# Mamba scan over its own decays in PSUM, with some multiplications by C moved to GpSimd

## Chip, cores and metric

The kernel runs on one core of a Trainium2 chip. The metric is the device time of one execution in microseconds. A core has five engines that run their own instruction queues in order and meet through semaphores: TensorE (PE), VectorE (DVE), ScalarE (ACT), GpSimd (POOL) and SyncE (SP, which issues DMAs here). Data lie in SBUF or in PSUM, the matmul output buffer.

## The reference, cut to what matters

The model is a tower of four blocks. The first is a three-layer Mamba beside a bidirectional LSTM, on 64 sequences of S = 33 tokens with D = 128 features. The inner width is 256 channels, so two halves of 128 partitions, and each channel has 16 states. For every layer:

```python
def step(h, inp):
    dt_t, B_t, C_t, u_t = inp
    dA = jnp.exp(dt_t[..., None] * A)
    h = dA * h + (dt_t * u_t)[..., None] * B_t[:, None, :]
    y = jnp.einsum('bcn,bn->bc', h, C_t)
    return (h, y)
```

Then `y + u * Dp`, times `silu(z)`, through `out_proj` and a layer norm. The other blocks (expert feed-forward layers, attention, a state space layer, an LSTM mixture of experts) are not touched by the change.

## The kernel before

All of this is in `mamba_lstm` (L389). The 64 sequences of a layer are cut into five items of 13, 13, 13, 13 and 12 sequences (858 or 792 columns for both channel halves together), so three layers make 15 items, j = 0 to 14. Each item goes through its 16 states, k = 0 to 15, and g = 16 j + k counts states over the whole loop, 240 of them. For one state:

- ScalarE computes the decays dA = exp(dt * A) into one of two PSUM buffers, `dA[:, g % 2]`, in two activations, one for each half (`decay`, L1036). It writes columns 1 to 32 of each sequence; column 0 holds a zero from one memset at the start (L1280), which restarts the recurrence at each sequence. Decay g waits for scan g - 2 (`h_ready`), which frees the buffer.
- GpSimd computes dBu = du * B into one of two SBUF buffers (L1346), also after scan g - 2.
- VectorE runs the recurrence over all columns in one `tensor_tensor_scan` from dA and dBu into `hst`, a ring of HR = 5 SBUF buffers (`scan`, L1251), and multiplies that buffer in place with C (`weigh`, L1261). Both operands of the multiplication lie in SBUF. The order on VectorE is scan(g), weigh(g - 1), scan(g + 1), weigh(g) and so on.
- TensorE adds the product into `py` in PSUM with two identity matmuls (`add`, through the helper line L573). A scan that reuses a ring buffer waits for the addition five states earlier.

B and C rows, replicated over the partitions, come by DMA from SP's queue, two states at a time, in rings of NBS = 4 buffers. A buffer of C is loaded again when `weighed` shows that its states are done.

Other work is written out by hand between the states, by the value of k. On VectorE: `soften` (L1193, L1196, L1201: e, dt, du of item j + 1) and `back` (L1215) at k = 8, `gate` (L1209, yz) at k = 1, the LSTM's `lstm_c` (L1223, L1225, L1228: ig, act3, cz) at k = 1, 5, 9 and `lstm_h` (L1235) at k = 2, 6, 10. On ScalarE, in this order within a state: decay(g), then `lstm_cell` (tc = tanh(c), L1018, at k = 3, 7, 11, which waits for VectorE's cz), `lstm_gates` (k = 2, 6, 10), `lstm_keep` (k = 4, 8, 12), the softplus steps of item j + 1, the layer norm, and `project`, which at k = 11 loads the SiLU tables (L876), runs three SiLUs (L878, L880, L882) for item j + 2 and loads the exponential's tables again (L883). The LSTM runs three time steps in each of the items 1 to 11 (`LSTM_ITEMS` = 11), so items 12 to 14 have no LSTM work, and items 13 and 14 no `project`. The GpSimd loop has dBu alone, beside eight small weight products (L1320); at k = 10 it waits for `soften` and `back`.

The order of VectorE's and ScalarE's loops around the change:

```python
for g in range(NI * DST):
    j, k = g // DST, g % DST
    scan(g)
    if g >= 1:
        weigh(g - 1)
```

Of the kernel before, what the change touches and what calls it, by code (L numbers as in the profile page):

```python
# [10 lines left out]
ALU = mybir.AluOpType  # L11
ACT = mybir.ActivationFunctionType
# [3 lines left out]
S = 33  # L16
# [356 lines left out]
LOG_KAPPA = -26 * 0.6931471805599453  # L373
PER_ITEM = 3
LSTM_ITEMS = S // PER_ITEM


def item(j):
# [5 lines left out]
def by_seq(ap):  # L384

    return ap.rearrange("p (b s) -> p b s", s=S)


def mamba_lstm(nc, cst, consts, mdct_dram, frames_dram, w_dram, cw_dram, lstm_dram, xn, m, hT):  # L389

    with ExitStack() as ctx:
        def sb(name, shape, dt=F32):
            return sbuf(nc, ctx, name, shape, dt)
# [5 lines left out]
        wop = sb("wop", [128, NL, 2, 128])  # L399
        negA = sb("negA", [128, NL, 2 * DST])  # L400
        edge = sb("edge", [128, 6])
        u = sb("u", [128, 2, 2, SCW])
        sz = sb("sz", [128, 3, 2, SCW])
        dt = sb("dt", [128, 2, 2, SCW])
# [39 lines left out]
                      "z_gated xd_ready xd_done rows_stored"))  # L444
        (d_ready, mag_ready, d_read, e_ready, capped, w_ready, sq_w_ready, ln_ready, low_logged, low_ready, high_ready, dt_done, du_done) = ctx.enter_context(
            stage(nc, "d_ready mag_ready d_read e_ready capped w_ready sq_w_ready ln_ready low_logged low_ready high_ready dt_done du_done"))
        (dA_zeroed, dBu_ready, dA_ready, h_ready, weighed, y_added, y_gated) = ctx.enter_context(
            stage(nc, "dA_zeroed dBu_ready dA_ready h_ready weighed y_added y_gated"))
        (wop_ready, wop_kept, cent_ready, cent_kept, sq_ready, var_ready, var_read, rstd_ready, m_scaled, m_done) = ctx.enter_context(
            stage(nc, "wop_ready wop_kept cent_ready cent_kept sq_ready var_ready var_read rstd_ready m_scaled m_done"))  # L450
        (diag_ready, bias_set, lw_ready, gates_ready, gated, prods_ready, c_ready, tc_ready, r_ready, hs_kept, fused, fused_added) = ctx.enter_context(
# [60 lines left out]
        @block.sync  # L512
        def _(sp):
            wih_d, whh_d, b_d, fw_d, fb_d = lstm_dram

            def load_cw(l):
                if l == 1:
                    sp.wait_ge(built_first, DCV)
                else:
                    sp.wait_ge(built, DCV * (l - 1))  # L520
                sp.dma_start(cw[:, :, :], cw_dram[l].unsqueeze(0).broadcast_to([128, DCV, DIN])).then_inc(cw_loaded, 16)

            def store(j):
                l, at, n = item(j)
                sp.wait_ge(xd_done, j + 1)
                sp.dma_start(bc_rows[j % 3, :, 0:n], xd[DTR:DTR + 2 * DST, j % 2, 0:n]).then_inc(rows_stored, 16)

            def rows(j, first, k):
                l, at, n = item(j)
                return bc_rows[j % 3, first + BG * k:first + BG * k + BG, 0:n].unsqueeze(0).broadcast_to([128, BG, n])  # L530

            def load_frames(c):
                per = NB // NCH
                sp.dma_start(blocks[:, c * per:(c + 1) * per, :],
                             frames_dram.rearrange("p (b s) -> p b s", b=NB)[:, c * per:(c + 1) * per, :]).then_inc(f_loaded[c], 16)

            sp.dma_start(mdct, mdct_dram.rearrange("p (k n) -> p k n", k=2)).then_inc(mdct_loaded, 16)
            load_frames(0)
            load_frames(1)
            sp.dma_start(w[:, 0, :], w_dram[0]).then_inc(w0_loaded, 16)  # L540
            sp.dma_start(cw[:, :, :], cw_dram[0].unsqueeze(0).broadcast_to([128, DCV, DIN])).then_inc(cw0_loaded, 16)
            load_frames(2)
            load_frames(3)
            for l in range(1, NL):
                sp.dma_start(w[:, l, :], w_dram[l]).then_inc(w_loaded, 16)
            for dst, src in ((wih[:, :, :, :].rearrange("p g d h -> p (g d h)"), wih_d), (lb[:, 0, :], b_d[0]), (lb[:, 1, :], b_d[1]),
                             (fw[:, :, :], fw_d), (fb[:, :], fb_d)):
                sp.dma_start(dst, src).then_inc(l_loaded, 16)
            sp.wait_ge(l_zeroed, 1)
            for d in range(2):  # L550
                sp.dma_start(whh[d * H2:(d + 1) * H2, :, d, :], whh_d[d]).then_inc(l_loaded, 16)
            store(0)
            for j in range(NI):
                l, at, n = item(j)
                for k in range(NGR):
                    if k == 0:
                        sp.wait_ge(rows_stored, 16 * (j + 1))
                    q = NGR * j + k
                    if q >= NBS:
                        sp.wait_ge(dBu_ready, BG * (q - NBS + 1))  # L560
                    sp.dma_start(Bs[:, q % NBS, :, 0:n], rows(j, 0, k)).then_inc(b_loaded[q % NBS], 16)
                    if q >= NBS:
                        sp.wait_ge(weighed, BG * (q - NBS + 1))
                    sp.dma_start(Cs[:, q % NBS, :, 0:n], rows(j, DST, k)).then_inc(c_loaded[q % NBS], 16)
                    if k == (1 if j else 2) and j + 1 < NI:
                        store(j + 1)
                    if k == 2 and j in (0, NSC):
                        load_cw(l + 1)

        @block.tensor  # L570
        def _(pe):
# [137 lines left out]
            def add(g):  # L709
                j, k = g // DST, g % DST  # L710
                l, at, n = item(j)
                if k == 0:
                    if j >= 1:
                        pe.wait_ge(y_gated, j)
                    else:
                        pe.wait_ge(z_gated, 1)
                    pe.wait_ge(u_gated, j + 1)
                    pe.wait_ge(diag_ready, 2 * (l + 1))
                    for h in range(2):
                        mm(py[:, h, 0:n], diag[:, l, h, :], u[:, j % 2, h, 0:n], start=True, stop=False)  # L720
                pe.wait_ge(weighed, g + 1)
                for h in range(2):
                    last = mm(py[:, h, 0:n], cst["ident"], hst[:, g % HR, h * n:h * n + n], start=False, stop=(k == DST - 1))
                last.then_inc(y_added, 1)
# [90 lines left out]
        def _(act):  # L815
# [211 lines left out]
            def decay(g):  # L1027
                j, k = g // DST, g % DST
                l, at, n = item(j)
                if k == 0:  # L1030
                    act.wait_ge(dt_done, j + 1)
                if g >= 2:
                    act.wait_ge(h_ready, g - 1)
                for h in range(2):
                    o = by_seq(dA[:, g % 2, h * n:h * n + n])[:, :, 1:S]
                    last = a(o, by_seq(dt[:, j % 2, h, 0:n])[:, :, 1:S], ACT.Exp,  # L1036
                             scale=negA[:, l, h * DST + k:h * DST + k + 1])
                last.then_inc(dA_ready, 1)
# [102 lines left out]
        def _(dve):  # L1141
# [102 lines left out]
            def scan(g):  # L1244
                j = g // DST
                l, at, n = item(j)
                if g >= HR:
                    dve.wait_ge(y_added, g - HR + 1)
                dve.wait_ge(dBu_ready, g + 1)
                dve.wait_ge(dA_ready, g + 1)  # L1250
                v.tensor_tensor_scan(hst[:, g % HR, 0:2 * n], dA[:, g % 2, 0:2 * n], dBu[:, g % 2, 0:2 * n], 0.0, ALU.mult,  # L1251
                                     ALU.add).then_inc(h_ready, 1)

            def weigh(g):
                j, k = g // DST, g % DST
                l, at, n = item(j)
                q = g // BG
                dve.wait_ge(h_ready, g + 1)
                dve.wait_ge(c_loaded[q % NBS], 16 * (q // NBS + 1))
                h = hst[:, g % HR, 0:2 * n].rearrange("p (a n) -> p a n", a=2)  # L1260
                v.tensor_tensor(h, h, Cs[:, q % NBS, k % BG, 0:n].unsqueeze(1).broadcast_to([128, 2, n]),  # L1261
                                ALU.mult).then_inc(weighed, 1)

            keep_tokens(0)
# [17 lines left out]
            for g in range(NI * DST):  # L1282
                j, k = g // DST, g % DST
                scan(g)
                if g >= 1:
                    weigh(g - 1)
                if j == 0 and k in (3, 7, 11):
                    scale_unit(2 + k // 4)
                if 1 <= j <= LSTM_ITEMS:
# [21 lines left out]
        def _(pool):  # L1311
            g_ = nc.gpsimd

            def build(l, r):
# [4 lines left out]
                    pool.wait_ge(x_ready, 2 * NSC * (l - 1))  # L1319
                g_.tensor_tensor(wt[:, l % 2, r, :], W(l, "wi", 0, DIN), cw[:, r, :], ALU.mult).then_inc(built, 1)  # L1320

            for at, value in enumerate((BELOW_ONE, KAPPA / 2, -KAPPA * KAPPA / 6, LOG_KAPPA, CAP, KAPPA * KAPPA / 12)):
                g_.memset(edge[:, at:at + 1], value).then_inc(edge_set, 1)
            g_.memset(whh[:, :, :, :], 0.0).then_inc(l_zeroed, 1)
            pool.wait_ge(w0_loaded, 16)
            pool.wait_ge(cw0_loaded, 16)
            for r in reversed(range(DCV)):
# [3 lines left out]
            for g in range(NI * DST):  # L1331
# [12 lines left out]
                if g >= 2:  # L1344
                    pool.wait_ge(h_ready, g - 1)
                g_.tensor_tensor(dBu[:, g % 2, 0:2 * n].rearrange("p (a n) -> p a n", a=2), du[:, j % 2, :, 0:n],  # L1346
                                 Bs[:, q % NBS, k % BG, 0:n].unsqueeze(1).broadcast_to([128, 2, n]), ALU.mult).then_inc(dBu_ready, 1)
                if j in (1, NSC + 1) and k in (2, 4, 6, 8):
                    build(l + 1, k // 2 - 1)

# [2762 lines left out]
```

## Time and profile before

| what | value |
|---|---|
| median of 3 runs | 2124.9 us (2123.95 to 2128.16) |
| the profiled execution's own time | 2123.37 us |
| its span, first to last instruction | 2121.5 us |
| granted TensorE clock, mean share | 0.943 |
| PE busy | 1841.3 us (87%) |
| DVE busy | 1634.3 us (77%) |
| ACT busy | 1323.1 us (62%) |
| POOL busy | 1015.5 us (48%) |
| scans (L1251), 240 | 458.3 us |
| multiplications with C (L1261), 240 | 247.3 us |
| dBu on GpSimd (L1346), 240 | 589.2 us |
| decays (L1036), 480 activations | 269.9 us |

The loop over the 240 states takes the span from about 35 us to 803 us. A timeline row gives the start in us, the duration in us, engine, line, operation, the tile written and the tiles read, the shape (partitions x elements), how many instructions were merged, and in brackets the idle time of the engine before it and what ended it. Consecutive instructions of one engine overlap a little at their ends, so the distance from start to start is shorter than the duration. A row of grouped instructions ends with busy us, mean ns of one, and the idle time ahead of the group.

### The profile page before, as it was taken

How to read it: one execution, taken by the hardware profiler on the slowest of the kernel's cores; microseconds unless marked ns; L12 is line 12 of the kernel's file. 1: busy time of each engine (PE TensorE's matmuls, PEld its weight loads, DVE VectorE, ACT ScalarE, POOL GpSimd, SP SyncE). 2: the span in 40 equal slices, each digit the busy share in tenths (PEclk: the TensorE clock that was granted, in tenths of full speed). 3: DMA queues.
4: the chain of work that ended last, by engine and by line, in shares of the span. 5: the costliest groups of instructions: out<-in, count | busy, mean ns of one | idle time of the engine just before them, and what ended most of it. 6: DMA issues, size and time to landing. Idle time of an engine off the chain costs nothing. (4 is left out here: it accounts for less than half of the span.)

```text
span 2121.5 us, 49383 instructions
## 1 busy us (share of the span) xinstructions
PE 1841.3 (87%) x19527; PEld 1346.4 (63%) x19527; DVE 1634.3 (77%) x2595; ACT 1323.1 (62%) x2681; POOL 1015.5 (48%) x782
## 2 busy tenths in 40 slices
PE   8899889898888778987878787897798799999999
PEld 4444444444443335445567787676776599999999
DVE  5999999999999994768475442546544689998996
ACT  6988887778876643123544444342646488888886
POOL 3787777777777881100037777200630133333333
PEclk9999999999999998997879999898988799999999
DMA  5444444444445441600148889303720411112000
GB/s 191 128 137 140 132 145 134 136 140 133 136 140 144 133 115 41 155 9 1 28 127 270 253 264 249 86 0 116 245 65 12 191 66 66 66 66 77 7 7 7
DMA packets 98037, 241.63 MB, mean 114 GB/s; under 512 B 15024, under 2 KB 48320, under 8 KB 95504
## 3 DMA queue, kind: packets, MB, share of 16 engines
q1 hardware_dynamic: 89120, 218.12, 33.4%
q0 software_dynamic: 7680, 15.74, 3.2%
q10 hardware_dynamic: 1008, 4.62, 0.6%
q8 instruction: 155, 2.54, 0.5%
q14 instruction: 74, 0.61, 0.1%
HBM read 226.25 MB, written 12.19 MB: 112 GB/s over the span
## 5 line engine op out<-in xcount | busy, mean ns | idle before, releaser
L1346 POOL TENSOR_TENSOR dBu<-du,Bs 128x858 f32<-128x858 f32 (+1 forms) x240 | 589.2, 2457 | 184.4 <-DVE hst L1251 95.0
L573 PE MATMUL py<-hst,ident 128*128 128x429 f32 (+1 forms) x960 | 405.9, 551 | 78.6 <-DVE hst L1261 78.3
L1251 DVE TENSOR_TENSOR_SCAN hst<-dA,dBu 128x858 f32<-128x858 f32 (+1 forms) x240 | 458.3, 1910 | 6.6 <-ACT dA L1036 4.0
L573 PEld LDWEIGHTS py<-hst,ident 128*128 128x128 f32 x960 | 178.1, 197 | 269.3 <-DVE hst L1261 150.4
L1036 ACT ACTIVATE dA<-dt,negA 128x416 f32<-128x416 f32 (+1 forms) x480 | 269.9, 596 | 115.2 <-DVE hst L1251 113.5
L3671 POOL TENSOR_TENSOR hm<-h,mw 128x264 f32<-128x264 f32 x128 | 89.8, 701 | 390.7 <-DVE h L3651 390.7
L1261 DVE TENSOR_TENSOR hst<-hst,Cs 128x858 f32<-128x858 f32 (+1 forms) x240 | 247.3, 1030 | 0.0
L3542 PE MATMUL pg<-xm,wi 128*128 128x66 f16 x6144 | 214.3, 195 | 8.2 <-issue 6.8
L3542 PE MATMUL pg<-hs,wh 128*128 128x66 f16 x6144 | 217.5, 194 | 2.9 <-issue 2.9
L3542 PEld LDWEIGHTS pg<-xm,wi 128*128 128x128 f16 x6144 | 201.6, 98 | 12.8 <-issue 7.5
L3542 PEld LDWEIGHTS pg<-hs,wh 128*128 128x128 f16 x6144 | 203.8, 98 | 6.5 <-issue 3.1
L3068 ACT ACTIVATE eh<-ph,wb 128x128 f32<-128x128 f32 x384 | 109.4, 368 | 133.5 <-PE ph L2941 133.5
L3592 ACT ACTIVATE pg<-bz 128x1188 f32<-128x1188 f32 x128 | 149.1, 1166 | 6.2 <-PE pg L3537 2.2
L3641 DVE TENSOR_TENSOR prod<-z 128x528 f32<-128x528 f32 x128 | 111.7, 873 | 16.7 <-ACT z L3602 16.3
L2910 POOL DMA_INDIRECT xi<-token_rows,take x96 | 93.5, 974 | 44.9 <-issue 40.3
L3006 DVE COPY yo<-po 128x128 f32<-128x128 f32 x96 | 28.0, 291 | 106.3 <-PE po L2951 106.3
L2915 POOL DMA_INDIRECT expert_rows<-yo,give x96 | 94.9, 988 | 30.7 <-issue 25.9
L2941 PE MATMUL ph<-xT,wb 128*128 128x128 f32 x768 | 104.5, 280 | 1.8 <-DVE xT L3000 1.8
L3601 ACT ACTIVATE z<-pg,scale 128x528 f32<-128x528 f32 x128 | 88.1, 688 | 24.1 <-PE pg L3542 23.1
L2951 PE MATMUL po<-wb,eh 128*128 128x128 f32 x768 | 102.0, 277 | 0.0
L2349 POOL DMA_INDIRECT xi<-token_rows,take x24 | 25.4, 1057 | 157.5 <-issue 156.2
L2941 PEld LDWEIGHTS ph<-xT,wb 128*128 128x128 f32 x768 | 95.3, 195 | 2.8 <-DVE xT L3000 2.8
(600 smaller groups left out, 3471.5 us busy)
## 6 DMA issues: line engine op xcount, KB each, us to landing
wb<-sf_w SPq DMA_DIRECT2D x96, 514.0 KB, 5.3
Bs<-bc_rows SPq DMA_DIRECT2D x96, 429.0 KB, 4.6
Cs<-bc_rows SPq DMA_DIRECT2D x96, 429.0 KB, 3.5
mw<-route_weights SPq DMA_DIRECT2D x8, 2112.0 KB, 10.0
wb<-gf_w SPq DMA_DIRECT2D x24, 514.0 KB, 4.9
Bs<-bc_rows SPq DMA_DIRECT2D x24, 396.0 KB, 5.2
Cs<-bc_rows SPq DMA_DIRECT2D x24, 396.0 KB, 4.3
mb<-route_masks SPq DMA_DIRECT2D x8, 1088.0 KB, 12.7
```

What stands on the lines that cost most here:

```text
L573: return nc.tensor.matmul(out, weight, moving, **kw)
L1036: last = a(o, by_seq(dt[:, j % 2, h, 0:n])[:, :, 1:S], ACT.Exp, scale=negA[:, l, h * DST + k:h * DST + k + 1])
L1251: v.tensor_tensor_scan(hst[:, g % HR, 0:2 * n], dA[:, g % 2, 0:2 * n], dBu[:, g % 2, 0:2 * n], 0.0, ALU.mult, ALU.add).then_inc(h_ready, 1)
L1261: v.tensor_tensor(h, h, Cs[:, q % NBS, k % BG, 0:n].unsqueeze(1).broadcast_to([128, 2, n]), ALU.mult).then_inc(weighed, 1)
L1346: g_.tensor_tensor(dBu[:, g % 2, 0:2 * n].rearrange("p (a n) -> p a n", a=2), du[:, j % 2, :, 0:n], Bs[:, q % NBS, k % BG, 0:n].unsqueeze( ...
L2915: pool.indirect_dma_start(ys, bass.IndirectOffsetOnAxis(ap=give[:, d:d + 1], axis=0), yo[:, d % UN, :], None).then_inc(given[d % UN][0], 16)
L2941: last = nc.tensor.matmul(ph[:, j % 2, f * ST:(f + 1) * ST], wb[:, j % UN, f * 128:(f + 1) * 128], xT[:, j % UN, :], start=True, stop=True)
L2951: last = nc.tensor.matmul(po[:, j % 2, 0:D], eh[:, j % 3, f, :], wb[:, j % UN, F + f * D:F + (f + 1) * D], start=(f == 0), stop=(f == FC - 1))
L3068: last = nc.scalar.activation(eh[:, j % 3, f, :], ph[:, j % 2, f * ST:(f + 1) * ST], act_fn, bias=wb[:, j % UN, W1 + W2 + f:W1 + W2 + f + 1])
L3542: return nc.tensor.matmul(pg[q][:, bank, c:c + CB], (wh if u else wi)[:, wp, q * HE + e, GO[z_] * D:(GO[z_] + 1) * D], rhs, start=False, s ...
L3592: a(pg[q][:, :, 0:PERB * CB], bz[:, q, :, :], ACT.Copy).then_inc(seeded[q], 1)
L3641: link(v.tensor_tensor(prod[:, q, :, :], z[:, q, 0:2, :], z[:, q, 3:5, :], ALU.mult))
```

## The change

Each state gets a kind. "S" stays as it was. In "D" the scan writes over its decays in PSUM, VectorE multiplies from there into the `hst` buffer directly after the scan, and ScalarE, before it writes the next decays into that buffer, waits for the multiplication and puts the zeros back with a copy of 26 elements for each partition. In "P" the scan writes `hst` as before and GpSimd multiplies it in place, after the dBu of two states later. Items 1 to 11 have D at k = 8, 9, 12, 13 and P at k = 10, 14. Items 12 to 14 repeat D, D, P over k = 2 to 13. All else is S, so there are 68 D, 34 P and 138 S. `weighed` now counts VectorE's multiplications and `weighed_pool` GpSimd's. TensorE's addition waits for the one that applies, SP's load of C for both.

```diff
+IN_LSTM = {8: "D", 9: "D", 10: "P", 12: "D", 13: "D", 14: "P"}
+
+def kind(g):
+    j, k = g // DST, g % DST
+    if j <= LSTM_ITEMS:
+        return IN_LSTM.get(k, "S") if j >= 1 else "S"
+    return "DPD"[k % 3] if 2 <= k < DST - 2 else "S"
...
@@ SP
-                        sp.wait_ge(weighed, BG * (q - NBS + 1))
+                        sp.wait_ge(weighed, by_vector(BG * (q - NBS + 1) - 1))
+                        if by_gpsimd(BG * (q - NBS + 1) - 1):
+                            sp.wait_ge(weighed_pool, by_gpsimd(BG * (q - NBS + 1) - 1))
...
@@ TensorE, add(g)
-                pe.wait_ge(weighed, g + 1)
+                if kind(g) == "P":
+                    pe.wait_ge(weighed_pool, by_gpsimd(g))
+                else:
+                    pe.wait_ge(weighed, by_vector(g))
...
@@ ScalarE, decay(g)
-                if g >= 2:
+                if g >= 2 and kind(g - 2) == "D":
+                    act.wait_ge(zero_set, 1)
+                    act.wait_ge(weighed, by_vector(g - 2))
+                    a(by_seq(dA[:, g % 2, 0:2 * SCW])[:, :, 0], zero[:, :], ACT.Copy)
+                elif g >= 2:
                     act.wait_ge(h_ready, g - 1)
...
@@ VectorE, scan(g)
-                if g >= HR:
+                if g >= HR and kind(g) != "D":
                     dve.wait_ge(y_added, g - HR + 1)
...
-                v.tensor_tensor_scan(hst[:, g % HR, 0:2 * n], dA[:, g % 2, 0:2 * n], dBu[:, g % 2, 0:2 * n], 0.0, ALU.mult,
+                o = dA[:, g % 2, 0:2 * n] if kind(g) == "D" else hst[:, g % HR, 0:2 * n]
+                v.tensor_tensor_scan(o, dA[:, g % 2, 0:2 * n], dBu[:, g % 2, 0:2 * n], 0.0, ALU.mult,
...
@@ VectorE, weigh(g)
-                v.tensor_tensor(h, h, Cs[:, q % NBS, k % BG, 0:n].unsqueeze(1).broadcast_to([128, 2, n]),
+                x = h
+                if kind(g) == "D":
+                    x = dA[:, g % 2, 0:2 * n].rearrange("p (a n) -> p a n", a=2)
+                    if g >= HR:
+                        dve.wait_ge(y_added, g - HR + 1)
+                v.tensor_tensor(h, x, Cs[:, q % NBS, k % BG, 0:n].unsqueeze(1).broadcast_to([128, 2, n]),
...
@@ VectorE, loop
                 scan(g)
-                if g >= 1:
+                if g >= 1 and kind(g - 1) == "S":
                     weigh(g - 1)
+                if kind(g) == "D":
+                    weigh(g)
...
@@ GpSimd
+            def weigh(g):
...
+                pool.wait_ge(h_ready, g + 1)
+                pool.wait_ge(c_loaded[q % NBS], 16 * (q // NBS + 1))
+                h = hst[:, g % HR, 0:2 * n].rearrange("p (a n) -> p a n", a=2)
+                g_.tensor_tensor(h, h, Cs[:, q % NBS, k % BG, 0:n].unsqueeze(1).broadcast_to([128, 2, n]),
+                                 ALU.mult).then_inc(weighed_pool, 1)
...
@@ GpSimd, loop, behind the dBu of state g
+                if g >= 2 and kind(g - 2) == "P":
+                    weigh(g - 2)
```

## Rows read from the trace of the kernel before

**Rows 1.** Busy time in a stretch of the loop: PE, PEld, DVE, ACT, POOL, clock, DMA.

```profile
300.00:400.00 100.00, 87.94 (x322) 45.16 (x323) 99.01 (x95) 78.90 (x150) 77.84 (x34) 0.97 0.44 133
```

**Rows 2.** Waits from 30 to 805 us: us in total, times, longest.

```profile
DVE hst L1251 <- ACT dA L1036: 4.0, 13, 0.6
DVE hst L1251 <- POOL dBu L1346: 2.1, 1, 2.1
```

**Rows 3.** VectorE's groups by shape, 30 to 805 us.

```profile
L1251 DVE TENSOR_TENSOR_SCAN hst<-dA,dBu 128x858 f32<-128x858 f32 x192 | 371.8, 1937 | 5.2 <-ACT dA L1036 2.8 <-POOL dBu L1346 2.1
L1261 DVE TENSOR_TENSOR hst<-hst,Cs 128x858 f32<-128x858 f32 x192 | 200.9, 1046 | 0.0
...
L1193 DVE TENSOR_TENSOR e<-pos,e 128x858 f32<-128x858 f32 x12 | 12.6, 1048 | 0.0
L1209 DVE TENSOR_TENSOR yz<-sz,py 128x858 f32<-128x858 f32 x12 | 12.6, 1046 | 1.1 <-PE py L573 0.8
...
L1225 DVE SCALAR_TENSOR_TENSOR pair_ps<-pair_ps,cz 128x64 f32<-128x64 f32 x33 | 7.4, 223 | 0.0
...
L1161 DVE TENSOR_TENSOR xn<-xn,rstd 128x429 f32<-128x429 f32 x2 | 4.5, 2267 | 0.0
```

**Rows 4.** VectorE's timeline in item 5, from scan 8 to the next scan 1.

```profile
319.83 1.94 DVE L1251 TENSOR_TENSOR_SCAN hst<-dA,dBu 128x858 f32<-128x858 f32 x1
321.69 1.03 DVE L1261 TENSOR_TENSOR hst<-hst,Cs 128x858 f32<-128x858 f32 x1
322.63 1.05 DVE L1193 TENSOR_TENSOR e<-pos,e 128x858 f32<-128x858 f32 x1
323.79 1.05 DVE L1196 TENSOR_TENSOR dt<-e,low 128x858 f32<-128x858 f32 x1
...
326.42 1.94 DVE L1251 TENSOR_TENSOR_SCAN hst<-dA,dBu 128x858 f32<-128x858 f32 x1
328.27 1.26 DVE L1261 TENSOR_TENSOR hst<-hst,Cs 128x858 f32<-128x858 f32 x1
329.46 0.21 DVE L1223 SCALAR_TENSOR_TENSOR ig<-pair_ps,cz 128x64 f32<-128x64 f32 x1
...
329.85 0.23 DVE L1228 SCALAR_TENSOR_TENSOR cz<-pair_ps,ig 128x64 f32<-128x64 f32 x1
329.99 1.93 DVE L1251 TENSOR_TENSOR_SCAN hst<-dA,dBu 128x858 f32<-128x858 f32 x1
...
336.04 1.94 DVE L1251 TENSOR_TENSOR_SCAN hst<-dA,dBu 128x858 f32<-128x858 f32 x1 [0.25 <-ACT dA L1036]
...
347.24 1.94 DVE L1251 TENSOR_TENSOR_SCAN hst<-dA,dBu 128x858 f32<-128x858 f32 x1
...
350.03 1.94 DVE L1251 TENSOR_TENSOR_SCAN hst<-dA,dBu 128x858 f32<-128x858 f32 x1
```

**Rows 5.** ScalarE's timeline in the same item, tanh(c) to decay 12.

```profile
330.10 0.26 ACT L1018 ACTIVATE tc<-cz 128x64 f32<-128x64 f32 x1 [0.57 <-DVE cz L1228]
330.38 1.28 ACT L876 ACT_TABLE_LOAD   x1
...
334.77 1.14 ACT L1036 ACTIVATE dA<-dt,negA 128x416 f32<-128x416 f32 x2
```

**Rows 6.** GpSimd's dBu: its group by shape, then three places of the timeline.

```profile
L1346 POOL TENSOR_TENSOR dBu<-du,Bs 128x858 f32<-128x858 f32 x192 | 477.7, 2490 | 152.0 <-DVE hst L1251 74.7 <-DVE m L1215 49.3 <-DVE du L1201 25.8
...
59.38 2.59 POOL L1346 TENSOR_TENSOR dBu<-du,Bs 128x858 f32<-128x858 f32 x1 [0.33 <-DVE hst L1251]
...
68.52 1.70 POOL L1346 TENSOR_TENSOR dBu<-du,Bs 128x858 f32<-128x858 f32 x1 [6.55 <-DVE du L1201]
...
710.80 5.32 POOL L1346 TENSOR_TENSOR dBu<-du,Bs 128x858 f32<-128x858 f32 x2 [0.85 <-DVE hst L1251]
```

**Rows 7.** VectorE's gate beside that pair of dBu.

```profile
714.31 1.04 DVE L1209 TENSOR_TENSOR yz<-sz,py 128x858 f32<-128x858 f32 x1
```

**Rows 8.** DMA issues of C: count, KB each, median us to landing.

```profile
Cs<-bc_rows SPq DMA_DIRECT2D x96, 429.0 KB, 3.5
```

More of the change, by code:

```diff
@@ L375, with by_vector, by_gpsimd @@
 LSTM_ITEMS = S // PER_ITEM
+IN_LSTM = {8: "D", 9: "D", 10: "P", 12: "D", 13: "D", 14: "P"}
[4 more added lines that the diff above has]
+    return "DPD"[k % 3] if 2 <= k < DST - 2 else "S"
+def by_vector(g):
+    return sum(kind(i) != "P" for i in range(g + 1))
+def by_gpsimd(g):
+    return sum(kind(i) == "P" for i in range(g + 1))
 def item(j):
@@ L401, in mamba_lstm @@
         edge = sb("edge", [128, 6])
+        zero = sb("zero", [128, 2 * SQ])
         u = sb("u", [128, 2, 2, SCW])
@@ L446, in mamba_lstm @@
             stage(nc, "d_ready mag_ready d_read e_ready capped w_ready sq_w_ready ln_ready low_logged low_ready high_ready dt_done du_done"))
-        (dA_zeroed, dBu_ready, dA_ready, h_ready, weighed, y_added, y_gated) = ctx.enter_context(
-            stage(nc, "dA_zeroed dBu_ready dA_ready h_ready weighed y_added y_gated"))
+        (zero_set, dA_zeroed, dBu_ready, dA_ready, h_ready, weighed, weighed_pool, y_added, y_gated) = ctx.enter_context(
+            stage(nc, "zero_set dA_zeroed dBu_ready dA_ready h_ready weighed weighed_pool y_added y_gated"))
         (wop_ready, wop_kept, cent_ready, cent_kept, sq_ready, var_ready, var_read, rstd_ready, m_scaled, m_done) = ctx.enter_context(
@@ L1320, in build @@
                 g_.tensor_tensor(wt[:, l % 2, r, :], W(l, "wi", 0, DIN), cw[:, r, :], ALU.mult).then_inc(built, 1)
+            def weigh(g):
+                j, k = g // DST, g % DST
+                l, at, n = item(j)
+                q = g // BG
+                pool.wait_ge(h_ready, g + 1)
[3 more added lines that the diff above has]
+                                 ALU.mult).then_inc(weighed_pool, 1)
             for at, value in enumerate((BELOW_ONE, KAPPA / 2, -KAPPA * KAPPA / 6, LOG_KAPPA, CAP, KAPPA * KAPPA / 12)):
@@ L1324, in _ @@
             g_.memset(whh[:, :, :, :], 0.0).then_inc(l_zeroed, 1)
+            g_.memset(zero[:, :], 0.0).then_inc(zero_set, 1)
             pool.wait_ge(w0_loaded, 16)
```

## Prediction

> **What bounds the kernel now.** I read the stretches of the span first. In the Mamba and LSTM part, about 35 to 803 us, VectorE is busy 99.01 of 100 us, ScalarE 79 and GpSimd 78 [rows 1]; the rest of the program is not touched. The waits of that part say how close the other engines are: the 240 scans waited 4.0 us for decays and 2.1 us for dBu in all [rows 2]. So VectorE's own instructions set the time, and the next question is what each costs. One state is a scan (1.94 us, 1.855 from start to next start) and a multiplication with C, the weighing (1.03 us, 0.945 to the next start) [rows 3, 4].
>
> The timeline of one LSTM item (j = 5) shows what stands just behind VectorE [rows 4]. The soften (e, dt, du) follows scan 8, so the scans after it can be counted. lstm_c (ig, act3, cz) follows scan 9 and the weighing of state 8; cz is ready at 330.08. Then come scan 10, weighing 9, lstm_h, scan 11, weighing 10, and scan 12 at 336.04, after 0.25 us of idling for its decays. ScalarE's row explains the idling [rows 5]: its queue takes tanh(c) as soon as cz is there (330.10), then a table load, three SiLUs, a second table load, and decay 12 at 334.77. From tanh(c) to scan 12 is 5.94 us, all ScalarE's. VectorE has 5.7 us of other work in that stretch now. **That stretch has no room**, and it recurs in all 11 LSTM items.
>
> **The change, part by part.** I write D for states whose scan goes to PSUM and is weighed at once, P for those weighed by GpSimd, S for unchanged ones. There are 11 x 4 + 3 x 8 = 68 D and 11 x 2 + 3 x 4 = 34 P.
>
> *Removed from VectorE:* 34 weighings, 34 x 0.945 = 32.1 us. *Added there:* a D weighing that follows its own scan has to wait for it. The trace has no such pair; the nearest is dt behind e, 1.16 us to the next start for 0.95 in free order [rows 4]. Ends 0.05 and 0.25 us, I take 0.15. Of the 68, 43 come straight behind their scan (k = 9, 13 of the LSTM items, seven in each of the last three): 6.5 us.
>
> *PSUM as operand.* No scan writes PSUM in the trace. The nearest rows: act3 is written to PSUM in 223 ns, its twin ig to SBUF in 0.21 us [rows 3, 4]; yz reads py in PSUM in 1046 ns, e from SBUF alone takes 1048 ns [rows 3]. So I take nothing; ends -0.05 and +0.1 us for a D state, -3 to +7 us. The Trainium skill (VectorE: DVE Perf Modes, the section on the TRN2 errata) gives a PSUM source 120 cycles of fixed cost against 58, some 0.065 us more, by which the sum would be 4.4 us higher, called an estimate; the yz row does not show that.
>
> *ScalarE:* 68 zeroings, 26 elements each. Nearest is tanh(c), 64 elements, 0.26 us [rows 5]; ends 0.1 and 0.26, I take 0.25. They lie under VectorE's work except where ScalarE is late. More weighty, the decay two states behind a D state now waits for its weighing too, 1.1 us later than before.
>
> *GpSimd:* 34 weighings of dBu's shape. Undisturbed, that takes 1.70 us [rows 6]; dBu's usual 2.49 holds a VectorE weighing that keeps it out. It works both ways: an xn multiplication of 429 columns took 2.27 us, while the dBu that began at 59.38 ran to 61.97 [rows 3, 6]. A dBu did not delay yz, which reads one operand from PSUM: 1.04 us at 714.31, inside the pair of dBu from 710.80 [rows 6, 7]. The Trainium skill (SBUF — State Buffer, Who interferes with whom) has this as a rule: a VectorE instruction with two SBUF inputs and a GpSimd instruction that reads SBUF exclude each other for their whole length. The trace agrees with it. So D weighings cost GpSimd nothing, S weighings can be held up by up to 1.70 us.
>
> *LSTM item, walked through* (j = 5, times as in rows 4, scan 8 held at 319.83). Weighings 7 and 8 now both stand ahead of the soften: scan 9 at 327.37 (was 326.42). Weighing 9 stands ahead of lstm_c: 327.37 + 1.855 + 0.15 + 0.945 puts lstm_c at 330.32 (was 329.46), cz at 330.95. ScalarE may begin decay 11 only when weighing 9 is done, 330.41; with zeroing and two exponentials tanh(c) starts at 331.77, not 330.97. Then the same 5.94 us: scan 12 at 337.71 (was 336.04). VectorE has only scan 10, lstm_h and scan 11 there, some 3.9 us, and **idles 3.0 us** instead of 0.25. The weighing of state 10 that was taken away is therefore worth nothing.
> After scan 12: four scans, weighings 11, 12, 13 and one 0.15, 10.41 us, where it was 11.20. Next item's scan 0 could start at 348.12. GpSimd has from scan 14's end (346.35): dBu of the next state 0 (to 348.2), weighing 14 (to 349.9), dBu of state 1 (to 351.6). Weighing 15, behind scan 0, wants the port at 350.2 and waits till 351.6; next scan 1 starts at 352.5 (was 350.03), **+2.5 us**. If weighing 15 got in first, dBu of state 1 would end near 352.9 and scan 1 be as late, so the order matters little. The gates that lstm_c then needs come at about 354.7, before its 355.3. Eleven items: 27.5 us. In about half of them weighing 8 was not held up as here (1.26 us [rows 4]) and the loss is 0.24 larger; I leave that in the range.
>
> *Last three items.* Per triple D, D, P: three scans, two weighings, two times 0.15, 7.75 us for 8.39. GpSimd needs 6.8 of it, ScalarE's tightest decay is ready 0.2 us early. Per item 4 x 0.945 - 7 x 0.15 = 2.7 us gained. Against it: at k = 8 GpSimd's weighing 7 holds the port 0.7 us into the soften; at the end of items 12 and 13 GpSimd has dBu 15, weighing 13, dBu 0 in a row, and weighing 14 waits for it, 1.6 us; in item 12 decay 11, the SiLU block (4.4 us from the first table load to decay 12 [rows 5]) and decay 12 end 7.1 us after scan 10 starts, while two scans and weighing 11 fill 4.8, 2.3 us of stall. Sum: +1.9, -0.4, -1.5, near 0.
>
> *Queues behind the new waits.* TensorE's addition of state 10 comes after GpSimd's weighing, at 336.3; the x_proj matmuls behind it are needed by ScalarE only after decay 14, at about 342.9. Additions may be four states late before a scan waits; the longest lag here is two. SP waits for both counters before a C load; the buffers are four pairs of states deep, over 20 us, a load lands in 3.5 us [rows 8]. No DMA is added. All three at nothing.
>
> **Sum:** +27.5 us on the profiled execution's 2123.4 (span 2121.5), so 2150.9; the median of the runs shown is 2124.9, 1.5 us more, in the noise. I say 2151.
>
> **Rivals.** (a) *VectorE stays the only bound* (other side). ScalarE's block would have to start before cz and GpSimd's chain to end in time: then 32.1 - 6.5 = 25.6 us are gained, 2099. For it speaks that VectorE is 99% busy and that scans hardly wait. It decides where a scan 12 waits under 0.5 us. Against it stand rows 5 and the order of the code. Chance 0.1.
> (b) *Only ScalarE's block binds*, GpSimd's weighings and the port cost nothing: scan 12 is 1.67 late, 0.79 comes back, 0.9 x 11 = 9.7, and the last items gain 7.9 - 2.3 = 5.6: +4, 2128. For it: GpSimd's chain is built from one 1.70 us row and margins of 0.3 us. Chance 0.2; half of it within no change.
> (c) *The port is lost twice.* When dBu of state 1 ends, dBu of state 2 is already free to run (scan 0 is over), and if GpSimd goes first, the waiting weighing waits another 1.70 us, in 11 + 2 places: +22, 2173. The xn row shows VectorE waiting for one dBu only (2.27 for 0.6 us of work). Chance 0.08.
> (d) *The change doesn't do what it says*: the compiler or chip makes a scan over its own PSUM input slower, for instance by its 1.94 us becoming 2.2: +18 us in the 68 D states, some of it inside the stalls, 2165. Chance 0.04.
>
> **How the numbers follow.** My case has 0.58. Its own range: zeroing 0.1 for 0.25, the 0.15 as 0.05, a quarter of GpSimd's losses gone, give 2139; the unblocked weighing 8 and PSUM at +0.1 give 2161. To hold 8 in 10 the range reaches from (b)'s low side, 2123, to 2166, which leaves out (a), most of (c) and a little of the rest. About 0.2% (4.2 us, 2120.7 to 2129.1) is what a measurement of this kernel can tell from no change. Faster: (a) and a tail of (b), 0.13. Same: half of (b) and little else, 0.12. Slower: 0.75.
>
> **What the profile of the changed kernel would show.** Scan 12 of each LSTM item waits near 3 us for decays, about 30 us over all; tanh(c) starts about 0.8 us after cz; VectorE's busy time falls by some 32 us less what blocked weighings add, and its share in these stretches from 99 to about 92%; the weighing of state 15 takes near 2.4 us in LSTM items, that of state 14 in items 12 and 13; dBu falls to 1.7 us behind D states; D scans stay at 1.94 and D weighings at 1.03. I am wrong if scan 12 waits under 1 us, if scans wait for dBu for more than 10 us in all, or if D scans are slower.

## The result, and the profile after

The changed kernel takes 2163.7 us (median of 4 runs, 2161.64 to 2168.01) against 2125.8 us. The ratio is 1.0176 with a 95% interval of 1.0162 to 1.0191, so it is slower by 37.4 +- 3 us. The forecast was +27.5 us, with 2123 to 2166 us as its range. The profiled execution took 2161.64 us, with a span of 2159.8. Two executions of the experiments below (7124 us in e13, 2948 us in e14) were slow ones and count in no median or ratio.

To see what belongs to the change I cut the span at VectorE's gate, the instruction that writes yz, once in each item. From the first gate to the twelfth are the 11 LSTM items. They take 599.31 us where they took 567.72: **+31.6 us, 2.87 an item**. The last three items take +1.3. What is left of the span's difference, 2.8 us ahead of the first gate and 2.6 us behind the last, lies where both programs issue the same work but for one small memset of zeros. Over the 12 experiments below these two stretches scattered from -1.5 to +3.0 and from -5.5 to +9.1 us. In this execution TensorE's granted clock was 0.66 between 40 and 50 us, where it had been 1.00, and ScalarE waited for it (2.35 and 2.26 us in two places, where it had waited 0.83 and 1.08). So the change accounts for 32.9 us of the profile, and the medians alone can't say more than their interval.

Busy time in one stretch of the loop (columns as in [rows 1]):

```profile
500.00:600.00 100.00, 85.64 (x333) 45.49 (x332) 92.06 (x86) 78.58 (x158) 70.36 (x34) 0.95 0.43 126
```

VectorE is busy for 92.06 of these 100 us, where it was for 98.25 in the same stretch before. From the first gate to the twelfth its share has fallen from 98.8 to 93.2%. The waits say for whom (30 to 850 us, they answer to [rows 2]):

```profile
PE py L595 <- POOL hst L1366: 69.1, 20, 4.8
...
DVE dA L1281 <- ACT dA L1065: 34.5, 13, 3.0
...
DVE hst L1281 <- POOL dBu L1394: 5.3, 10, 2.1
...
DVE yz L1238 <- PE py L595: 3.9, 7, 1.1
```

The scans wait 38.0 us for decays in all (34.5 in the row above for D scans, 3.5 for S and P scans), where they had waited 4.0. 31.3 of it are eleven waits at one place, scan 12 of the LSTM items. The groups show that the operands in PSUM cost nothing and what the port costs (they answer to [rows 3, 6]):

```profile
L1281 DVE TENSOR_TENSOR_SCAN hst<-dA,dBu 128x858 f32<-128x858 f32 x140 | 269.6, 1933 | 9.0 <-POOL dBu L1394 4.9 <-ACT dA L1065 3.5
L1296 DVE TENSOR_TENSOR hst<-hst,Cs 128x858 f32<-128x858 f32 x114 | 135.4, 1188 | 0.0
L1281 DVE TENSOR_TENSOR_SCAN dA<-dA,dBu 128x858 f32<-128x858 f32 x52 | 101.0, 1943 | 27.4 <-ACT dA L1065 27.4
...
L1296 DVE TENSOR_TENSOR hst<-dA,Cs 128x858 f32<-128x858 f32 x52 | 54.4, 1046 | 1.1
```

A scan into PSUM takes 1943 ns against 1933 into SBUF, a D weighing 1046 ns, which is what an S weighing took before. The S weighings have gone from 1046 to 1188 ns on average: GpSimd keeps some of them out, and that time counts as busy. So VectorE's busy time has fallen by only 6.4 us over the program (1634.3 to 1627.9), though 34 weighings of 0.945 us are gone. ScalarE's and GpSimd's groups:

```profile
L1060 ACT ACTIVATE dA<-zero 128x26 f32<-128x26 f32 x68 | 13.3, 196 | 145.7 <-DVE hst L1296 145.7
```

```profile
L1394 POOL TENSOR_TENSOR dBu<-du,Bs 128x858 f32<-128x858 f32 x192 | 425.8, 2222 | 190.7 <-DVE hst L1281 78.2 <-DVE m L1244 47.1 <-DVE du L1230 34.9
...
L1366 POOL TENSOR_TENSOR hst<-hst,Cs 128x858 f32<-128x858 f32 x26 | 47.7, 1835 | 0.0
```

Now item 5, the one that the prediction walked through. VectorE's timeline, from the soften to the next scan 1 (it answers to [rows 4]):

```profile
337.90 1.04 DVE L1222 TENSOR_TENSOR e<-pos,e 128x858 f32<-128x858 f32 x1
...
341.68 1.95 DVE L1281 TENSOR_TENSOR_SCAN dA<-dA,dBu 128x858 f32<-128x858 f32 x1
343.66 1.05 DVE L1296 TENSOR_TENSOR hst<-dA,Cs 128x858 f32<-128x858 f32 x1
344.63 0.22 DVE L1252 SCALAR_TENSOR_TENSOR ig<-pair_ps,cz 128x64 f32<-128x64 f32 x1
...
345.01 0.22 DVE L1257 SCALAR_TENSOR_TENSOR cz<-pair_ps,ig 128x64 f32<-128x64 f32 x1
...
351.89 1.95 DVE L1281 TENSOR_TENSOR_SCAN dA<-dA,dBu 128x858 f32<-128x858 f32 x1 [2.84 <-ACT dA L1065]
...
362.81 1.95 DVE L1281 TENSOR_TENSOR_SCAN hst<-dA,dBu 128x858 f32<-128x858 f32 x1 [0.43 <-POOL dBu L1394]
364.67 2.46 DVE L1296 TENSOR_TENSOR hst<-hst,Cs 128x858 f32<-128x858 f32 x1
367.04 1.93 DVE L1281 TENSOR_TENSOR_SCAN hst<-dA,dBu 128x858 f32<-128x858 f32 x1
```

And ScalarE's (it answers to [rows 5]):

```profile
344.81 0.20 ACT L1060 ACTIVATE dA<-zero 128x26 f32<-128x26 f32 x1 [4.21 <-DVE hst L1296]
344.94 1.12 ACT L1065 ACTIVATE dA<-dt,negA 128x416 f32<-128x416 f32 x2
346.00 0.24 ACT L1043 ACTIVATE tc<-cz 128x64 f32<-128x64 f32 x1
346.26 1.28 ACT L901 ACT_TABLE_LOAD   x1
...
350.65 1.14 ACT L1065 ACTIVATE dA<-dt,negA 128x416 f32<-128x416 f32 x2
```

Read them together. ScalarE idles 4.21 us, as decay 11 may not begin before weighing 9, which ends at 344.71. cz is there at 345.23, tanh(c) starts at 346.00, and scan 12 comes 5.89 us after that, as before. From the soften's start to scan 12 are 13.99 us (the prediction's own times give 14.13). At the end of the item GpSimd has three operations in a row:

```profile
360.71 2.01 POOL L1394 TENSOR_TENSOR dBu<-du,Bs 128x858 f32<-128x858 f32 x1 [1.17 <-DVE hst L1281]
362.67 1.73 POOL L1366 TENSOR_TENSOR hst<-hst,Cs 128x858 f32<-128x858 f32 x1
364.34 4.34 POOL L1394 TENSOR_TENSOR dBu<-du,Bs 128x858 f32<-128x858 f32 x2
```

The first of the two dBu that the last row holds has the port from 364.34, when weighing 15 is issued at 364.67. The weighing then takes 2.46 us, where it took 1.03 before.

### The profile page after: what moved, and what is told of

The parts are those of the page before. It is cut to its first block and busy times, and to the rows that moved or that the text cites. A ratio compares the mean times of both kernels' runs of the same rounds, so it can differ in the third digit from the quotient of the medians.

```text
span 2159.8 us, 49625 instructions
## 1 busy us (share of the span) xinstructions
PE 1853.8 (86%) x19527; PEld 1351.3 (63%) x19527; DVE 1627.9 (75%) x2561; ACT 1328.9 (62%) x2749; POOL 1006.9 (47%) x817
## 5 line engine op out<-in xcount | busy, mean ns | idle before, releaser
L1394 POOL TENSOR_TENSOR dBu<-du,Bs 128x858 f32<-128x858 f32 (+1 forms) x240 | 522.4, 2181 | 231.6 <-DVE hst L1281 98.3
L595 PEld LDWEIGHTS py<-hst,ident 128*128 128x128 f32 x960 | 183.7, 199 | 267.9 <-issue 114.1
L1281 DVE TENSOR_TENSOR_SCAN hst<-dA,dBu 128x858 f32<-128x858 f32 (+1 forms) x172 | 326.9, 1907 | 9.5 <-POOL dBu L1394 5.3
L1296 DVE TENSOR_TENSOR hst<-hst,Cs 128x858 f32<-128x858 f32 (+1 forms) x138 | 161.6, 1171 | 0.0
L1281 DVE TENSOR_TENSOR_SCAN dA<-dA,dBu 128x858 f32<-128x858 f32 (+1 forms) x68 | 129.9, 1910 | 34.5 <-ACT dA L1065 34.5
L2960 POOL DMA_INDIRECT xi<-token_rows,take x96 | 93.7, 976 | 45.1 <-issue 39.0
L1060 ACT ACTIVATE dA<-zero 128x26 f32<-128x26 f32 x68 | 13.3, 196 | 145.7 <-DVE hst L1296 145.7
```

Of the source, the lines that this page charges most:

```text
L595: return nc.tensor.matmul(out, weight, moving, **kw)
L1281: v.tensor_tensor_scan(o, dA[:, g % 2, 0:2 * n], dBu[:, g % 2, 0:2 * n], 0.0, ALU.mult, ALU.add).then_inc(h_ready, 1)
L1296: v.tensor_tensor(h, x, Cs[:, q % NBS, k % BG, 0:n].unsqueeze(1).broadcast_to([128, 2, n]), ALU.mult).then_inc(weighed, 1)
```

## The experiments

Theory: the loss is a matter of order. A D weighing ahead of lstm_c, and the decay behind it that tanh(c) is queued behind, make ScalarE's SiLU block late, and GpSimd's chain behind k = 14 adds to it. Rivals: each D or P state has a price; or the port is the whole of it; or TensorE. Every run changes `IN_LSTM` or the line for the last items, unless a diff says otherwise. "11 items" and "last 3" are the gate to gate differences to the kernel before, in us, from each run's profile. They repeat to 0.1 us where the code in the stretch and just ahead of it is the same, much finer than the whole time; with other code ahead of them, the same last three items came to +1.9 in e1 and +1.3 here. The ratios are to the executions of the kernel before that were taken beside each run, whose median lay between 2125.8 and 2127.9 us, and are not quotients of two medians.

| run | median us | ratio to before, 95% | 11 items | last 3 |
|---|---|---|---|---|
| changed kernel | 2163.7 | 1.0176, 1.0162 to 1.0191 | +31.6 | +1.3 |
| e1 last items only | 2130.5 | 1.0016, 1.0003 to 1.0030 | -0.1 | +1.9 |
| e2 LSTM items only | 2158.1 | 1.0140, 1.0123 to 1.0157 | +31.6 | 0.0 |
| e13 one D state, k = 9 | 2143.2 | 1.0094, 1.0057 to 1.0131 | +18.0 | 0.0 |
| e5 k = 9 back | 2145.4 | 1.0089, 1.0067 to 1.0110 | +17.8 | +1.2 |
| e3 k = 10 back | 2157.5 | 1.0137, 1.0108 to 1.0167 | +31.6 | +1.3 |
| e4 k = 14 back | 2156.0 | 1.0129, 1.0109 to 1.0148 | +30.4 | +1.4 |
| e10 k = 15 as D | 2154.3 | 1.0138, 1.0121 to 1.0156 | +31.1 | +1.4 |
| e7 D only, no P | 2163.4 | 1.0173, 1.0153 to 1.0193 | +30.5 | +3.9 |
| e12 e4, delta earlier | 2156.0 | 1.0133, 1.0104 to 1.0163 | +25.2 | +1.5 |
| e8 other states | 2127.9 | 1.0006, 0.9988 to 1.0024 | -1.8 | -0.6 |
| e14 P at 6 and 12 | 2124.7 | 0.9994, 0.9976 to 1.0013 | -3.7 | 0.0 |
| e11 P at 6 alone | 2120.2 | 0.9972, 0.9957 to 0.9987 | -4.7 | 0.0 |

**Where it sits: e1 and e2.**

```diff
-IN_LSTM = {8: "D", 9: "D", 10: "P", 12: "D", 13: "D", 14: "P"}
+IN_LSTM = {}
```

```diff
-    return "DPD"[k % 3] if 2 <= k < DST - 2 else "S"
+    return "S"
```

> Items 1 to 11 all S, items 12 to 14 as in the changed kernel. The theory (the loss comes from the order ahead of lstm_c at k = 9 and from GpSimd's chain behind k = 14, in LSTM items): the 11 x 2.87 us of the LSTM items go, the last three keep their +1.3, so +1 us on before, 2127, and 4 us more only if the slow TensorE clock near 45 us belongs to the change. Rival 1 (each D or P state has a price of its own, 37.9 us over 102 states): 36 states, +13 us, 2139. Rival 2 (VectorE alone is the bound): 12 weighings less 21 x 0.15, -8 us, 2118.

> Items 12 to 14 all S, LSTM items as in the changed kernel. The theory: +31.6 us on before, and up to 5 for the clock, 2157 to 2162. Rival 1 (a price of each state): 66 states, +24.5 us, 2150.

36 of the 102 changed states cost 1.9 us and 66 cost 31.6, so there is no common price of a state: rival 1 of these expectations falls, and so does rival 2, VectorE alone as the bound (2118 us for e1). The last items also gain nothing.

**One D state: e13 and e5.**

```diff
-IN_LSTM = {8: "D", 9: "D", 10: "P", 12: "D", 13: "D", 14: "P"}
+IN_LSTM = {9: "D"}                                        # e13, last items S
+IN_LSTM = {8: "D", 10: "P", 12: "D", 13: "D", 14: "P"}    # e5
```

> Only k = 9 of items 1 to 11 is D, all else S, nothing on GpSimd. The theory: one D state at this place puts its weighing (0.95 us) ahead of lstm_c and lets decay 11, which tanh(c) stands behind, begin 1.1 us later; scan 12 comes 1.75 us later and VectorE, which has no less to do, idles about 2.0 us there: 11 x 1.75 = +19 us on before, 2147. Rival (the loss grows with the number of D and P states): 11 of 102, +4 us.

> In LSTM items k = 9 is S again, so weighing 9 stands behind lstm_c and scan 10, and decay 11 waits for the scan only. The theory: lstm_c starts 1.1 us earlier, tanh(c) 1.36 us earlier (held by decay 11), scan 12 too: 11 x 1.36 = -15 us on the changed kernel, 2149; scan 12 waits about 1.7 us. Rival (scan 12's wait comes from missing VectorE work alone, whatever is ahead of lstm_c): the order makes no difference, 0 to +2 us.

A single D state in an item, with no instruction taken from VectorE and none given to GpSimd, costs 18.0 us in the 11 items (19 expected). Taking it out of the changed kernel gives 13.8 back (15 expected). In e13 VectorE's timeline of item 8 has

```profile
499.12 0.22 DVE L1257 SCALAR_TENSOR_TENSOR cz<-pair_ps,ig 128x64 f32<-128x64 f32 x1
...
503.07 1.16 DVE L1296 TENSOR_TENSOR hst<-hst,Cs 128x858 f32<-128x858 f32 x1
506.02 1.94 DVE L1281 TENSOR_TENSOR_SCAN hst<-dA,dBu 128x858 f32<-128x858 f32 x1 [1.78 <-POOL dBu L1394]
```

and ScalarE's has

```profile
500.10 0.24 ACT L1043 ACTIVATE tc<-cz 128x64 f32<-128x64 f32 x1
...
504.75 1.14 ACT L1065 ACTIVATE dA<-dt,negA 128x416 f32<-128x416 f32 x2
```

The row names GpSimd as the releaser, and that is a trap. The dBu that scan 12 reads is the one before the last and had ended at 503.33; decay 12 ended at 505.89, and the scan followed 0.13 us later. Reading the queue gives the cause that the name hides.

**The weighing taken away at k = 10: e3.**

```diff
+IN_LSTM = {8: "D", 9: "D", 12: "D", 13: "D", 14: "P"}
```

> In LSTM items k = 10 is S again, so VectorE weighs it. The theory: scan 12's wait falls from 2.84 to 1.9 us, exactly what the weighing takes, and the time is that of the changed kernel, 2163 +- 2. Rival (the weighing taken away was a gain, the loss is elsewhere): 11 x 0.945 = +10.4 us, 2174.

The 11 items take 31.6 us more either way. Scan 12's wait falls from 2.83 to 1.75 us in item 8, and from 31.3 to 20.4 over the eleven, as a weighing of 0.945 us (held up a little, 1.17 in item 8) fills it. The 10.4 us that this part of the change takes from VectorE are worth nothing. The median is 6 us lower than the changed kernel's, while these items and the last three take the same to 0.1 us, so that difference isn't this edit's.

**GpSimd's chain: e4, e10, e7.**

```diff
+IN_LSTM = {8: "D", 9: "D", 10: "P", 12: "D", 13: "D"}                        # e4
+IN_LSTM = {8: "D", 9: "D", 10: "P", 12: "D", 13: "D", 14: "P", 15: "D"}      # e10
+IN_LSTM = {8: "D", 9: "D", 12: "D", 13: "D"}                                 # e7
+    return "DSD"[k % 3] if 2 <= k < DST - 2 else "S"                         # e7
```

> In LSTM items k = 14 is S again. The theory: weighing 15 falls from 2.46 to 1.03 us, weighing 14 is back with 0.945, and the gates of the next item, which ScalarE ends at the same time as before, allow about 0.6 us an item: -7 us on the changed kernel, 2157. Rival (GpSimd's weighing costs VectorE nothing): +10.4 us, 2174.

> In LSTM items k = 15 is D too: its weighing reads PSUM and can't be kept out by GpSimd. The theory: the 2.46 us weighing is 1.05, but the next scan 1 then waits about 0.6 us for GpSimd's dBu, which ends as late as ever: -0.7 us an item, -7 us on the changed kernel, 2157. Rival (the port is the whole of this loss): -1.3 us an item, -14 us, 2150.

> All P states are S again, the D states stay. The theory: D states alone bring most of the loss, by the order ahead of lstm_c and ScalarE's later decays: 11 x 1.95 in LSTM items, +3 in the last ones, +24 us on before, 2150; D scans 1.94 us, D weighings 1.05. Rival (the loss is GpSimd's and the port's): within 5 us of before, 2126 to 2131.

Here the theory missed. Without the chain the items should have been 7 us shorter, and are 1.2 (e4) and 0.5 (e10) shorter. In e10 weighing 15 does fall to 1.05 us, and scan 1 then waits for GpSimd's dBu in every item, 0.93 us on average where 0.6 had been expected. e7, with no weighing on GpSimd at all, was expected at +24 us and came at +34.4 by its profile (30.5 and 3.9). So the rival by which the port is the whole of the loss falls. The 2.46 us weighing is gone in e4, but something else has taken its place. TensorE's timeline of e4, end of item 8:

```profile
524.93 0.99 PE L595 MATMUL pair_ps<-xd,w 65*128 65x429 f32 x2 [0.87 <-ACT pos L923]
525.75 1.61 PE L595 MATMUL py<-hst,ident 128*128 128x429 f32 x4
527.29 1.14 PE L595 MATMUL pair_ps<-xn,wih 128*64 128x64 f32 x16
528.36 1.10 PE L595 MATMUL pair_ps<-hr,whh 128*128 128x64 f32 x8
529.30 1.66 PE L595 MATMUL py<-hst,ident 128*128 128x429 f32 x4
530.80 0.88 PE L595 MATMUL pair_ps<-m,cen 128*128 128x429 f32 x2
531.52 1.60 PE L595 MATMUL pair_ps<-yz,wop 128*128 128x429 f32 x4
532.96 1.60 PE L595 MATMUL py<-hst,ident 128*128 128x429 f32 x4
```

and VectorE's gate:

```profile
534.60 1.05 DVE L1238 TENSOR_TENSOR yz<-sz,py 128x858 f32<-128x858 f32 x1 [1.48 <-PE py L595]
```

TensorE runs without a gap from 524.93 to the last addition, which the gate waits for. It could not begin earlier: the second delta matmul (xd,w) waits for `pos`, which stands behind decay 15 on ScalarE, and decay 15 waits for the D weighing of state 13. Such waits of the gate come to 9.9 us in the 11 items of e4 and e7 and 9.6 in e10, against 0.8 before and 2.6 in the changed kernel, where GpSimd's chain lies nearly as late and hides the rest.

**TensorE's chain put to the test: e12.** In e4, with ScalarE's Abs and Relu ahead of decay 15:

```diff
+                if k == 15 and j + 2 < NI:
+                    steps(j + 2, k)
                 if g >= 5:
                     decay(g)
...
                 if k == 15:
-                    if j + 2 < NI:
-                        steps(j + 2, k)
+                    pass
```

> The kernel with k = 14 back on VectorE (e4), and ScalarE's Abs and Relu of the next delta moved from behind decay 15 to ahead of it. The theory: in e4 the gate waits 1.5 us for TensorE, whose second delta matmul waits for that Relu, with all additions behind it; it then starts 1.4 us earlier, scan 15 waits 0.5 us more, the gate comes 1.0 us earlier: -11 us on e4, 2145. Rival (the gate's wait is TensorE's own amount of work): no change, or +5 by scan 15.

The gate's wait for TensorE is gone, from 9.9 us to none, and the 11 items are 5.3 us shorter: half of the 11 expected. The expectation had taken the 1.48 us of item 8 for every item, where the mean is 0.90. Scan 15 waits 6.4 us in all for its later decay (0.58 an item, 0.5 expected). In item 8 TensorE's last addition now ends at 530.26 us, and the gate follows at once, so there is little left to gain at this place:

```profile
530.30 1.05 DVE L1239 TENSOR_TENSOR yz<-sz,py 128x858 f32<-128x858 f32 x1
```

So the queue behind `pos` was the cause of the gate's wait; TensorE's amount of work (the rival) was not. The whole time doesn't show it (1.0133 against 1.0129): this run spent 5.4 us more than e4 behind the last gate.

**The same mechanism where there is room: e8, e11, e14.**

```diff
+IN_LSTM = {6: "P", 7: "D", 8: "D"}                     # e8
+IN_LSTM = {6: "P", 7: "D"}                             # e11, last items S
+IN_LSTM = {6: "P", 7: "D", 12: "P", 13: "D"}           # e14, last items S, and e12's edit
```

In e8 the last items have P at 3 and 6 and D at 4, 5, 7 and 8; items 13 and 14 have P at 10 and D at 9 and 11 as well.

> The same mechanism in other places: in LSTM items P at k = 6 and D at 7, 8; in items 12 to 14 P at 3, 6 (and 10 in items 13, 14) with D behind them, nothing at k = 9 to 15 of LSTM items and nothing before the SiLU block of item 12. The theory: each P gives 0.945 - 0.3 = 0.64 us, 19 of them, and weighing 8 is no longer held up: -13 us on before, 2113. Rival (GpSimd's weighings always give the time back through the port or the decays): at or above before, 2126 to 2135.

> P at k = 6 and D at k = 7 of the LSTM items only, k = 8 left S, so that its weighing still stands between scan 9 and lstm_c and covers decay 11. The theory: 0.945 - 0.15 - 0.2 = 0.6 us an item without a later wait, -6.5 us on before, 2120; the wait of scan 12 stays at 0.25 (it was 0.8 in e8, where weighing 8 had gone ahead). Rival: 0.1 to 0.3 us an item as in e8.

> As e11, with P at k = 12 and D at k = 13 too, and ScalarE's Abs and Relu ahead of decay 15. The theory: P at 12 comes behind the SiLU block, so VectorE gains another 0.4 us an item (GpSimd's third operation in a row keeps scan 15 from more), and TensorE gets its delta early enough: 11 x 1.0 = -11 us on before, 2115. Rival (TensorE or ScalarE takes it back at the gate of the next item): as e11 or slower than before.

e8 gave nothing measurable where 13 us were expected. The cause stands in one row of VectorE's timeline:

```profile
492.51 1.95 DVE L1284 TENSOR_TENSOR_SCAN hst<-dA,dBu 128x858 f32<-128x858 f32 x1 [0.80 <-ACT dA L1068]
```

With state 8 as D its weighing has moved ahead of the soften, and lstm_c follows scan 9 directly. Decay 11, which can start only after scan 9, now ends later than cz, so tanh(c) waits for it, and 0.55 us of the gain are lost. e11 leaves state 8 alone. The same row is there again with 0.24 us, as before the change, the items are 4.7 us shorter, and the kernel is **faster than both, 0.9972 (0.9957 to 0.9987), 6 us** (6.5 expected; 0.43 us an item by the profile, as the soften's first step is held up 0.4 us on average by GpSimd's weighing, not 0.2). e14 added a P behind the SiLU block, together with e12's edit. By the medians it lost what e11 had; by the gates it kept 3.7 of the 4.7 us, and the rest of the difference lies behind the last gate, outside the changed code. Of the further gain that was expected nothing came:

```profile
502.45 1.95 DVE L1282 TENSOR_TENSOR_SCAN hst<-dA,dBu 128x858 f32<-128x858 f32 x1 [0.63 <-POOL dBu L1395]
...
511.73 1.05 DVE L1239 TENSOR_TENSOR yz<-sz,py 128x858 f32<-128x858 f32 x1 [0.60 <-PE py L595]
```

GpSimd's three operations in a row hold scan 15, by 7.1 us over the eleven items where e11 has none; decay 15 had ended at 501.72 and the dBu at 502.37, so this time the name in the row is the right one. TensorE holds the gate, 2.6 us against 0.9 in e11. The rival was right in what came of it ("as e11 or slower"), and only in the smaller part in why: it had named the gate, not GpSimd. As two edits were made at once, what the second did here is not shown.

## Why the prediction was right, and what it had too small

- **The SiLU block** (VectorE "idles 3.0 us instead of 0.25"): right, 2.84 us in the item walked through, 2.73 to 3.00 in all eleven. e13 and e5 show the cause, e3 that weighing 10 was worth nothing.
- **GpSimd's chain and the port**: the row is as forecast (weighing 15 in 2.46 us, near 2.4 said; 0.43 us of wait at scan 0, 0.2 said). From the soften to the next scan 1, 29.14 us; the prediction's times give 28.92. The remark that the order of weighing 15 and dBu matters little was borne out by chance: in item 2 of e2 the weighing got in first (1.03 us), scan 1 then waited 1.82 us for its dBu, and the item lost 2.94 us where it loses 2.92 in the changed kernel. But e4 and e10 show that taking this part away gives back only 1.2 and 0.5 us of the 31.6.
- **The failed step** is "Queues behind the new waits", where TensorE was taken "at nothing". I had compared single additions with the ring of `hst`, and not followed TensorE's queue to the gate, which waits for all of them. In the changed kernel this adds 1.8 us (the gate's waits, 2.6 against 0.8). It also made the losses parallel: taking one away leaves the others, which is why e4 and e7 missed. e7's expectation had 11 x 1.95 = 21.5 us for these items, measured are 30.5, and the gate's waits have grown by 9.1. So the number of the changed kernel is in part luck: the loss that the prediction gave to GpSimd's chain is there, but with a shorter chain the queue left out of the sum would have cost nearly as much.
- **The size.** 2.5 an item was walked through, 2.87 measured. The walked item had weighing 8 held up before the change; where it was not (five items), the loss is the 0.24 us larger that I had left in the range, 1.2 us. With TensorE's 1.8 that makes 30.5 of the 31.6 us. The last items were at +1.3 and not 0: by gates +2.28, -0.20, -0.79 (+1.9, -0.4, -1.5 forecast), scan 12 of item 12 waiting 2.11 us for 2.3. The rest of the 37.4, some 4.5 us, lies outside the changed code and was not forecast; the runs show scatter of that size there.
- **Prices.** The chained D weighing costs 0.12 us (1.98 from its scan's start for 1.855; 0.15 taken), the zeroing 196 ns (0.25 taken), PSUM operands nothing. The 0.065 us that were estimated for a PSUM source from the Trainium skill (VectorE: DVE Perf Modes, the section on the TRN2 errata) do not show: 1046 ns from PSUM, 1046 from SBUF. The Trainium skill's rule on the shared port (SBUF — State Buffer, Who interferes with whom) holds: S weighings behind GpSimd are stretched, up to 2.77 us, and no D weighing took over 1.05 us.
- **Rivals.** (a), VectorE alone as the bound, would have needed scan 12 to wait under 0.5 us, and e3 excludes it. (b), ScalarE's block alone, needed GpSimd's weighings and the port to cost nothing, and weighing 15 took 2.44 to 2.77 us in every item; even with them gone from there (e4) or from everywhere (e7), the time is far above its 2128. (c), the port lost twice, did not happen: one GpSimd operation of wait each time. (d) fell with the 1943 ns of the D scans.

## What to carry to other kernels

An engine that is 99% busy need not be the only bound: ask which instruction of it feeds another engine's queue, and count what stands ahead of that instruction, not only what the engine has to do in all. An instruction taken away behind such a point gives idle time; one moved ahead of it costs its full length, and more if it also holds back something in the other queue. When several engines end within a microsecond of each other at a meeting point, taking one delay away shows the next, so follow each queue to the meeting point before any of them is called free.

## What the runs showed of the hardware that was not expected

TensorE waited 4.76 us for GpSimd's weighing of state 10 in item 8, and then ran near half speed for some microseconds. Its stretches (columns as in [rows 1]), with no such dip at the same place of the item before the change (granted clock 1.00 from 491 to 503 us):

```profile
512.50:517.50 5.00, 0.28 (x1) 0.00 (x0) 2.86 (x3) 4.94 (x8) 3.96 (x3) 0.85 0.67 153
517.50:523.50 6.00, 5.96 (x9) 2.11 (x10) 5.31 (x4) 4.04 (x11) 4.15 (x2) 0.56 0.20 59
523.50:531.00 7.50, 7.44 (x35) 3.88 (x34) 7.45 (x6) 6.26 (x14) 5.85 (x4) 1.00 0.60 179
```

```profile
517.54 3.23 PE L595 MATMUL py<-hst,ident 128*128 128x429 f32 x4 [4.76 <-POOL hst L1366]
```

The granted clock was 0.56 from 517.5 to 523.5 us, near the lower of its two levels (1.2 of 2.4 GHz), after 5 us in which TensorE was busy for 0.28. Four matmuls of 429 columns took 3.23 us; in e4, later in the item, four took 1.61. So a wait can slow TensorE twice, by itself and by the clock after it. It need not be GpSimd that makes it wait. In e3 and e7 VectorE weighs state 10, and because D states weigh early, its queue holds no other weighing between 9 and 10. TensorE waits 3.72 us there, and its clock falls as well (0.55 from 513.79 to 519.50 us in e3):

```profile
513.79 3.23 PE L595 MATMUL py<-hst,ident 128*128 128x429 f32 x4 [3.72 <-DVE hst L1296]
```

That the slow stretch cost the changed kernel time does not show. In e3 it begins 1.0 us earlier against scan 12, and TensorE then stands idle 0.87 us for `pos`; the second delta matmul comes 9.07 us after scan 12 starts in e3 and 9.06 us in the changed kernel, and both have the same +31.6 us and the same 2.6 us of waits at the gate.
